# Running sums of an attention layer: carried in PSUM as float32r parts, and taken along one sequence

## The reference

```python
pos_values = x @ Wpv + bpv
pos_mem_cos = cumsum(cos(pp) * pos_values, axis=1)          # pp: phases of the position, the same for both sequences
pos_mem_sin = cumsum(sin(pp) * pos_values, axis=1)
pos_ret = (cos(pp) * pos_mem_cos + sin(pp) * pos_mem_sin) / sqrt(D)
key_ph = tanh(x @ Wk + bk) * pi
gates = sigmoid(gelu(concat([x, shift1(x)]) @ Wg1 + bg1) @ Wg2 + bg2)
kv_mem_cos = cumsum(shift1(cos(key_ph)) * (x @ Wkv + bkv) * gates, axis=1)
kv_mem_sin = cumsum(shift1(sin(key_ph)) * (x @ Wkv + bkv) * gates, axis=1)
kv_ret = (cos(key_ph) * kv_mem_cos + sin(key_ph) * kv_mem_sin) / (sqrt(max(cumsum(gates), 1)) * sqrt(D))
blended = bw[0] * pos_ret + bw[1] * kv_ret                   # bw: softmax of a small network of x
out = x + layernorm(blended) @ Wo + bo                       # x here: layernorm of the input; then
x1 = x_in + layernorm(out)                                   # ... the layer's residual
```

## Time and profile before

| | |
|---|---|
| median of 3 runs | 3562.35 us |
| the profiled execution | 3565.71 us, of which its span 3563.9 us |
| PE busy in the span | 3177.3 us (89%) |
| DVE busy | 3086.5 us (87%) |
| ACT busy | 2120.2 us (59%) |
| POOL busy | 1935.4 us (54%) |
| first phase | from 0 to about 799.5 us of the span |

### The profile page before, as it was taken

The page is one execution under the profiler, slowest core; times in us unless marked ns, Lnnn a source line. Parts: engine busy times, 40 slices in busy tenths (PEclk is TensorE's granted clock), DMA queues, the critical chain, the costliest instruction groups (busy, mean ns, idle before and its releaser), DMA issues. The chain is left out here.

```text
span 3563.9 us, 91251 instructions
## 1 busy us (share of the span) xinstructions
PE 3177.3 (89%) x31284; PEld 2733.0 (77%) x31284; DVE 3086.5 (87%) x15020; ACT 2120.2 (59%) x4411; POOL 1935.4 (54%) x1758
## 2 busy tenths in 40 slices
PE   5999999972599999999999999999999999999988
PEld 3666666642488888888888888888888888888878
DVE  5666666656999999999999999999999999999971
ACT  3444444422666666666666766666666666766662
POOL 1333333333466666556556666666556656666664
PEclk9999999986699988988888999889998888999988
DMA  2111111103333333333333333333333333333332
GB/s 64 48 54 54 54 54 54 42 30 133 141 117 117 116 105 114 122 105 105 105 105 118 125 119 119 117 108 105 124 112 105 105 105 115 124 124 117 114 117 95
DMA packets 132328, 356.85 MB, mean 100 GB/s; under 512 B 13865, under 2 KB 61609, under 8 KB 129452
## 3 DMA queue, kind: packets, MB, share of 16 engines
q1 hardware_dynamic: 131868, 351.03, 30.3%
HBM read 309.01 MB, written 25.17 MB: 94 GB/s over the span
## 5 line engine op out<-in xcount | busy, mean ns | idle before, releaser
L1209 PE MATMUL b_ps_a<-b_wup,b_hid 128*128 128x256 f32 x4096 | 955.8, 379 | 1.5 <-POOL b_hid L1023 1.5
L1198 PE MATMUL b_ps_h<-b_xT_hi,b_wd_split 128*128 128x256 f32 x4096 | 931.9, 311 | 22.7 <-ACT b_hid L1349 22.5
L1209 PEld LDWEIGHTS b_ps_a<-b_wup,b_hid 128*128 128x128 f32 x4096 | 744.3, 190 | 85.7 <-POOL b_hid L1023 1.7
L1023 POOL TENSOR_TENSOR b_hid<-b_hid,b_gates 128x512 f32<-128x512 f32 x512 | 661.9, 1295 | 197.8 <-ACT b_hid L1349 197.8
L1198 PEld LDWEIGHTS b_ps_h<-b_xT_hi,b_wd_split 128*128 128x128 f32 x4096 | 703.5, 200 | 38.3 <-issue 27.9
L1328 ACT ACTIVATE b_ohq<-b_q_no,b_minus_qid 80x128 f16<-80x128 f16 x2048 | 648.7, 391 | 1.0
L1004 POOL TENSOR_SCALAR b_rstd<-b_mv 128x2 f32<-128x2 f32 x64 | 136.4, 2131 | 860.8 <-DVE b_mv L1388 860.8
L1123 PE MATMUL b_ps_s<-b_ohr,b_ohq 80*128 80x32 f16 x16384 | 452.6, 185 | 167.1 <-issue 125.5
L1198 PE MATMUL b_ps_h<-b_xT_lo,b_wd_split 128*128 128x256 f32 x2048 | 596.9, 291 | 0.0
L1123 PEld LDWEIGHTS b_ps_s<-b_ohr,b_ohq 80*128 80x128 f16 x16384 | 443.8, 102 | 176.0 <-issue 132.3
L1349 ACT ACTIVATE b_hid<-b_ps_h 128x512 f32<-128x512 f32 x512 | 303.8, 593 | 371.5 <-PE b_ps_h L1198 371.3
(11 more groups left out here) (192 smaller groups left out, 5508.8 us busy)
## 6 DMA issues: line engine op xcount, KB each, us to landing
b_wd_split<-wd_parts SPq DMA_DIRECT2D x512, 512.0 KB, 3.8
a_keysh<-a_key SPq DMA_DIRECT2D x16, 896.0 KB, 5.4
a_x<-in_x SPq DMA_DIRECT2D x16, 512.0 KB, 4.9
x_between<-a_y SPq DMA_DIRECT2D x16, 512.0 KB, 3.2
b_x<-x_between SPq DMA_DIRECT2D x32, 256.0 KB, 2.7
wd_parts<-b_wd_split SPq DMA_DIRECT2D x16, 512.0 KB, 2.9
b_x1t<-x_between SPq DMA_DIRECT2D x32, 256.0 KB, 5.5
out<-b_y SPq DMA_DIRECT2D x32, 256.0 KB, 5.6
```

The lines of the kernel that those rows point to most:

```text
L1023: G.tensor_tensor(hid[:, p % 4, :, :], hid[:, p % 4, :, :], gates[:, 2 * p:2 * p + 2, :], ALU.mult).then_inc(mix_done, 1)
L1198: mm = T.matmul(hbank[p % 2][:, j * C:(j + 1) * C], a, c, start=i == 0, stop=i == len(parts) - 1)
L1209: mm = T.matmul(abank[:, t * D:(t + 1) * D], hid[:, p % 4, j, t * P:(t + 1) * P], wup[:, 2 * p + j, :], start=p == 0 and j == 0 and t == 0 ...
```

## The change

- The sums stay in PSUM along a sequence. For each tile `sums` adds to `cbank` first the rows that the tile before left out (`rest`, the matrix ones - tri, times that tile's terms), then its own (`upto`, a copy of tri): together these make the running sum. Both are float32r, and so are the terms, in two parts: `u_hi`, made on ACT by `high_terms` (a copy of 128x1024), and `u_lo` = u - u_hi, made on POOL by `low_terms`. That makes 8 float32r matmuls of 512 columns for a tile (4 for the first of a sequence) in place of 4 float32 ones. `keep_carry` and `carry` go; `back` now waits for `sums` itself.
- The chunks go along sequence 0 and then sequence 1. The phases are loaded, reduced and turned into sines for every chunk instead of every second one.
- The first values and terms of the next chunk, `values(n + 1, 0)` and `terms(n + 1, 0)`, stand ahead of `sums(n, 3)` and `back(n, 3)`. `norm_out` and `add_input` of chunk n - 2 stand early in the loop's turn n (they stood at the end of turn n - 1). `reduce_phases(n + 1)` stands behind `back(n, 0)`; on SP the phases of chunk n + 1 are loaded behind the load of x for chunk n + 2. Some smaller steps move too: `norm_in`, `moments_in`, the second half of `gate_values` (now `gate_shares`), `turn_blend` ahead of `key_waves` on ACT.

The diff, cut to its core (new semaphores, the changed indices of slots, and the waits that only follow from them are left out):

```diff
-        for b in range(seqs):
-            G.memset(keysh[0:1, b, 0, :, :], 0.0)
-        G.memset(zeros[:, :], 0.0)
-        G.memset(carry[:, :, :], 0.0).then_inc(constants, 1)
+        G.memset(key_end[:, :, :, :], 0.0)
+        G.memset(zeros[:, :], 0.0).then_inc(constants, 1)
...
-        j, b = divmod(n, seqs)
+        b, j = divmod(n, per_seq)
...
         def load_phases(n):
-            j = n // seqs
-            if n % seqs == 0:
-                if j:
-                    sp.wait_ge(cs_done, j)
+            j = n % per_seq
+            if n:
+                sp.wait_ge(cs_done, n)
...
             if has(n + 2):
                 if n + 2 > 0:
                     load(n + 2)
-                load_phases(n + 2)
             if has(n + 1):
+                load_phases(n + 1)
                 shift_keys(n + 1)
             if has(n - 1):
                 store(n - 1)
...
+        def low_terms(n, t):
+            g = n * TA + t
+            i = g % 2
+            pool.wait_ge(u_hi_done, g + 1)
+            G.tensor_tensor(u_lo[:, i, :], u[:, i, :], u_hi[:, i, :].bitcast(F32), ALU.subtract).then_inc(u_lo_done, 1)
...
-        for n in range(-2, chunks + 1):
+        for n in range(-2, chunks + 2):
+            if has(n):
+                low_terms(n, 1)
+            if has(n - 2):
+                add_input(n - 2)
             if has(n - 1):
                 root(1, n - 1)
             if has(n):
                 gather_terms(n, 0)
+                low_terms(n, 2)
             if has(n + 2):
                 root(0, n + 2)
             if has(n):
                 gather_terms(n, 1)
+                low_terms(n, 3)
                 gather_terms(n, 2)
+            if has(n + 1):
+                low_terms(n + 1, 0)
             if has(n - 1):
                 root(2, n - 1)
             if has(n):
                 gather_terms(n, 3)
             if has(n + 1):
                 gate_root(n + 1)
-            if has(n - 1):
-                add_input(n - 1)
...
         def sums(n, t):
-            pe.wait_ge(u_done, g + 1)
+            first = g % (per_seq * TA) == 0
+            pe.wait_ge(upto_done, 1)
             if g:
                 pe.wait_ge(prod_done, g)
-            for h in range(2):
-                mm = T.matmul(cbank[h][:, :], tri[:, :], u[:, i, h * 512:(h + 1) * 512], start=True, stop=first)
             if not first:
                 for h in range(2):
-                    mm = T.matmul(cbank[h][:, :], last_row[:, :], carry[:, b, h * 512:(h + 1) * 512], start=False, stop=True)
+                    for part in (u_hi, u_lo):
+                        mm = T.matmul(cbank[h][:, :], rest[:, :], part[:, (g - 1) % 2, h * 512:(h + 1) * 512], ...)
+                mm.then_inc(rest_pe, 1)
+            pe.wait_ge(u_lo_done, g + 1)
+            for h in range(2):
+                for part in (u_hi, u_lo):
+                    mm = T.matmul(cbank[h][:, :], upto[:, :], part[:, g % 2, h * 512:(h + 1) * 512], ...)
             mm.then_inc(sums_pe, 1)
...
     PE:   values(n, 1); turn_x(n + 1); sums(n, 0); keys(n + 1); values(n, 2); sums(n, 1); values(n, 3);
           gating(n + 1); turn_blend(n - 1); logits(n + 1); sums(n, 2); project_out(n - 1);
+          values(n + 1, 0);
           sums(n, 3); gate_sums(n + 1)
...
     ACT:  turn_x(n + 1);
-          keep_carry(n, 0); keys(n + 1); keep_carry(n, 1); gating(n + 1); key_waves(n + 1); turn_blend(n - 1);
-          gate_exp(n + 1); keep_carry(n, 2); keep_carry(n, 3); waves(n + 1)
+          high_terms(n, 1); keys(n + 1); high_terms(n, 2); gating(n + 1); turn_blend(n - 1); key_waves(n + 1);
+          high_terms(n, 3); gate_exp(n + 1); waves(n + 1); high_terms(n + 1, 0)
...
     DVE, of the changed kernel:
+          terms(n, 1); turn_x(n + 1); blend(n - 1, 3); norm_out(n - 2); gate_factors(n); blend_moments(n - 1);
+          back(n, 0); reduce_phases(n + 1); blend_norm(n - 1); terms(n, 2); moments_in(n + 2); back(n, 1);
+          blend(n, 0); terms(n, 3); norm_in(n + 2); blend(n, 1); gate_values(n + 1); back(n, 2);
+          gate_shares(n + 1); blend(n, 2); project_out(n - 1); terms(n + 1, 0); back(n, 3); gate_sums(n + 1)
```

More of the change, by code:

```diff
@@ L52, in attention_phase @@
     T, V, S, G = nc.tensor, nc.vector, nc.scalar, nc.gpsimd
-    chunks = seqs * length // CA
+    per_seq = length // CA
+    chunks = seqs * per_seq
     ident, tri, last_row, ones = (sb(f"a_{n}", [P, P]) for n in ("ident", "tri", "last_row", "ones"))
+    upto, rest = (sb(f"a_{n}", [P, P], F32R) for n in ("upto", "rest"))
     wproj = sb("a_wproj", [P, 2, KD, 3 * D], F32R)
@@ L88, in attention_phase @@
     u = sb("a_u", [P, 2, 4 * D])
-    carry = sb("a_carry", [P, seqs, 4 * D])
+    u_hi, u_lo = (sb(f"a_{n}", [P, 2, 4 * D], F32R) for n in ("u_hi", "u_lo"))
     prod = sb("a_prod", [P, 2, 2, 2, D])
@@ L138, in attention_phase @@
         sem(f"a_{n}") for n in ("w_high", "xT_hi", "x_before", "tanh", "th_abs", "key"))
[L139 to L143, removed]
+    hidden_done, exp_done, u_hi_done, lnT_done, ph_abs_done, cs_done = (
+        sem(f"a_{n}") for n in ("hidden", "exp", "u_hi", "lnT", "ph_abs", "cs"))
+    xT_pe, keys_pe, hidden_pe, logits_pe, gcum_pe, values_pe, rest_pe, sums_pe, lnT_pe, wo_pe = (
+        sem(f"a_{n}_pe") for n in ("xT", "keys", "hidden", "logits", "gcum", "values", "rest", "sums", "lnT", "wo"))
     N_WEIGHTS = 16
@@ L545, in act_program @@
             if has(n):
-                keep_carry(n, 1)
+                high_terms(n, 2)
             if has(n + 1):
                 gating(n + 1)
-                key_waves(n + 1)
             if has(n - 1):
@@ L552, in act_program @@
             if has(n + 1):
+                key_waves(n + 1)
+            if has(n):
+                high_terms(n, 3)
+            if has(n + 1):
                 gate_exp(n + 1)
-            if has(n):
-                keep_carry(n, 2)
-                keep_carry(n, 3)
             if has(n + 1):
                 waves(n + 1)
+                high_terms(n + 1, 0)
     def dve_program(dve):
+        dve.wait_ge(weights_in, 16 * N_WEIGHTS)
+        V.tensor_copy(upto[:, :], tri[:, :])
+        V.tensor_tensor(rest[:, :], ones[:, :], tri[:, :], ALU.subtract).then_inc(upto_done, 1)
         dve.wait_ge(w_high_done, 1)
@@ L745, in norm_out @@
             op.then_inc(norm_done[2], 1)
-        for n in range(-2, chunks + 1):
+        for n in range(-2, chunks + 2):
             if has(n):
-                terms(n, 0)
                 terms(n, 1)
+            if has(n + 1):
+                turn_x(n + 1)
             if has(n - 1):
                 blend(n - 1, TA - 1)
-            if has(n + 1):
-                turn_x(n + 1)
+            if has(n - 2):
+                norm_out(n - 2)
             if has(n):
@@ L760, in dve_program @@
                 back(n, 0)
-            if has(n + 2):
-                moments_in(n + 2)
-                reduce_phases(n + 2)
+            if has(n + 1):
+                reduce_phases(n + 1)
             if has(n - 1):
@@ L773, in dve_program @@
                 terms(n, 3)
+            if has(n + 2):
+                norm_in(n + 2)
+            if has(n):
                 blend(n, 1)
@@ L778, in dve_program @@
                 back(n, 2)
+            if has(n + 1):
+                gate_shares(n + 1)
+            if has(n):
                 blend(n, 2)
@@ L781, in dve_program @@
                 project_out(n - 1)
+            if has(n + 1):
+                terms(n + 1, 0)
             if has(n):
@@ L785, in dve_program @@
                 gate_sums(n + 1)
-            if has(n - 1):
-                norm_out(n - 1)
     with nc.Block() as block:
```

97 lines of the change are left out of this document (49 added, 48 removed).

## The result

The changed kernel takes 3664.96 us (median of 4 runs, 3664.28 to 3672.38) against 3561.54 us (median of 4, 3560.12 to 3564.18) for the kernel before: a ratio of 1.0294, 95% interval 1.0276 to 1.0312. It is slower by 103 us; 3653 was predicted, with 3575 to 3705 as the range. Of the four executions of the kernel with the phases loaded earlier one took 3812.38 us at a mean granted clock of 0.749; it counts in no ratio.

The account below looks back on a forecast made before the run. TensorE bounds the first phase until a chain across other engines is longer. 13 turns at 7.9 make +103, start and end -12: 3656.7 us, 3.4 less against the median, 3653; range 3575 to 3705.

Parts of the forecast that it names:

- The saving on PE: Sums on PE: four tiles save 4 x 1.7 = 6.8 us a chunk, leaving 37.3 with the hole closed.
- Steps 2 to 6: Chain from the end of high_terms(n,3) to the first Gelu of gating(n+2): 9.6, 7.2, 5.7, 6.9 and 11.4 us.
- step 1: Third gating group on PE, then third Gelu, turn_blend, key_waves and high_terms(n,3) on ACT: 9.0 us.
- The term of the clock: PE at 1.2 GHz after idling: third gating group 1.5 us longer, turn_blend held up by 0.5.
- The other signs: Turns of 50 to 55 us; DVE idle for the phases in 13; ACT awaits terms, PE the Gelu, SP add_input.
- The lock: Ports shared by DVE and POOL: 0.7 us where low_terms(n+1,1) meets norm_out; as a rival 3700 to 3725, chance 0.12.
- step 4: On POOL gate_root, low_terms(n+1,1) and add_input(n-1): 5.7 us, together 31.5.
- The rival that wanted 57 to 59 a turn: Each low_terms on POOL holds DVE's steps up to 2.35 us, PE colder: 3700 to 3725, chance 0.12.
- Start and end: First norm_in -5.9 us, first turns at PE's pace -8 and -2, open latencies at the end +4: together -12.
- The transfer isn't waited for: Phases already there for DVE when back(n+1,0) ends: 43.4 us a turn, 3523 in all, chance 0.12.
- PE stays the bound: First phase at PE's pace, 37.3 to 38.5 us a turn: 3452 in all, chance 0.05.
- step 6: On DVE reduce_phases(n+2), blend_norm, terms(n+1,2), then on ACT high_terms(n+1,2), table load and Gelu: 11.4 us.

Follow-up runs that it names:

- the last experiment: Changed kernel with terms(n,2) and phases early, low parts on DVE, and gate_factors, gate_sums, low_terms(n,0) moved on DVE: 3479.17 us, 0.9767 to the kernel before.
- the last two kernels: Changed kernel with terms(n,2) and phases early, low parts on DVE: 3516.57 us; the same with gate_factors, gate_sums, low_terms(n,0) moved on DVE: 3479.17 us.
- both cuts: Changed kernel with SP's phases load ahead of the store and ACT's gating and key_waves ahead of high_terms(n,2): 3663.66 us, 1.0282 to the kernel before.

## Why the prediction was right, point by point

- *TensorE bounds the kernel before.* Held: less PE work gave 54 us there. That "less work there pays until a chain across the other engines is longer" decided the case: that chain was only 3 us behind.
- *The saving on PE.* Held. In the warm stream the eight float32r matmuls of a tile start 0.23 us apart (404.89 to 406.52), 1.87 us with the last, against 1.92 predicted and the 3.63 of the earlier trace rows. PE's 37.3 a turn shows in the last experiment. The saving was real and lay off the path.
- *Steps 2 to 6.* All five came out within 0.2 us in the turn of the table. But the measured steps hold their handoffs (0.08 from the end of ACT's cast at 453.61 to POOL's subtraction at 453.69), for which the prediction had 1.0 more: that term wasn't needed. It made up for a step 1 that was 0.6 too short, so that 53.4 against 53.34 is in part luck. The landing is 6.0 in the median (4.7 to 6.8) against 5.9 in the earlier trace rows; the wait for it occurs in 13 turns, as counted.
- *Step 1.* The term of the clock was the weakest. PE idles 4.3 ahead of the third gating group, which then takes 2.93 in place of 1.5, and the eight transposes 1.91 in place of 1.04; so far as predicted. Not foreseen: in half of the turns `logits` also runs at 1.2 GHz (its groups of four take 0.99 in place of 0.58), `sums(n,3)` stands behind it, and `high_terms(n,3)` waits 1.75 for its `rest` half (the row at 452.57). Those turns have 12.65 against 11.0, the others 10.3 to 10.8, and the mean, 11.6, hides it.
- *PE's idle time.* 14 us a turn was predicted, most of it ahead of the third gating group. It is some 10, as PE at the lower clock is busy for some 43 and not 37.3; 3.9 of it stand ahead of that group and 4.2, more than anywhere else, ahead of `sums(n,1)`, a wait that the prediction doesn't have. So the sign "PE below 80% busy" missed narrowly: 82% from 100 to 796 us (568.95 of 696), at a clock of 0.85. The other signs came.
- *The lock.* Taken as 0.7 on the path, which came out at 0.6 (step 4). For DVE it is much more: `norm_out` takes 3.44 beside `low_terms(n,1)` (1.38 for the like step in the earlier trace rows), and the 4-column copy 2.36 beside `add_input`:

```profile
415.77 3.44 DVE L618 TENSOR_SCALAR a_y<-a_y,a_mv,a_rstd 128x256 f32<-128x256 f32 x4
416.31 2.43 POOL L253 TENSOR_TENSOR a_u_lo<-a_u,a_u_hi 128x1024 fp32r<-128x1024 f32 x1
...
419.30 2.36 POOL L263 TENSOR_TENSOR a_y<-a_y,a_x 128x1024 f32<-128x1024 f32 x1 [0.55 <-DVE a_y L618]
419.33 2.36 DVE L667 COPY a_fac<-a_z 128x4 f32<-128x4 f32 x1
```

  The copy is issued 0.03 behind the addition and ends with it; alone it takes 0.17. In sum DVE is busy for 40 a turn where its work in the kernel before is 32. The rival that wanted 57 to 59 a turn for this fell all the same: these holds end ahead of the wait for the phases, and taking the largest away changed nothing. They cost once that wait is gone: the last two kernels lie 37 us apart, though the last also moves `gate_sums` and a subtraction, so that not all of it need be the holds. The Trainium skill, "SBUF — State Buffer", "Who interferes with whom", says that whoever issues first gets the shared ports for the whole instruction; these rows agree, and so does the first pair of the earlier trace rows; its last row, POOL's scaling of 128x256, stays the exception.
- *Start and end.* This term was mis-sized: -12 predicted, some -3 measured (98.6 of span, less 13 x 7.84 = 102); it is the larger part of the 12 us by which 3653 fell short. The first `norm_in` did come 6 us earlier (first `logits` done at 53.2 against 59.0 us), but I set the next turns, at PE's new pace, against 45.5 us. The kernel before has turns of 34.4 and 43.0 there itself (58.98, 93.43, 136.44, against 53.19, 91.19, 129.75), so that they gave 1 us in place of 8 to 10. And by the first store the lead of 7 us was gone (156.35 against 156.27): `norm_out` and `add_input` of a chunk now stand in the next turn, which the term doesn't count; that this took the lead is likely, and no run shows it. It was an average taken where it didn't hold.
- *The rivals.* "The transfer isn't waited for" and "PE stays the bound" are excluded by the wait in 13 turns and by the run with half of the sums. The order of the transfers is a cause: moving that issue alone gave back 67 us. But the rival's price for an unwaited transfer, 43.4 a turn, was too low: it was 47.8, as the other steps don't fall away with it.

My expectations behind the prediction were poorer where I cut the ring in one place and didn't walk the queues again: with the Gelus moved ahead I had 3530 to 3560 for both cuts, and got 3664.

One more row on the path: the table load ahead of the Gelu starts 0.02 us behind the end of the cast and takes 1.28, and the Gelu follows at once, at 440.27:

```profile
437.92 1.04 ACT L505 CAST a_u_hi<-a_u 128x1024 fp32r<-128x1024 f32 x1 [19.05 <-DVE a_u L633]
438.98 1.28 ACT L520 ACT_TABLE_LOAD   x1
```

The Trainium skill, "ScalarE: Activation LUTs", "What ACT_TABLE_LOAD costs", gives the load about 1.28 and a drain of about 1.38 beside it. By that step 6 would be 1.4 longer; the load agrees, and the trace shows no drain here.

What stays open: which link is the last one in the kernel with the early terms and phases (45.0 a turn), and whether the two lengths of turn would become one if PE were given work in its hole; neither was tried.

## What to carry to other kernels

When work on the fullest engine is replaced by smaller pieces that pass through three others, walk the ring from one event of a turn to the same event of the next, through every in-order queue and every transfer that waits behind it; if the walk is longer than a turn, the saving is not to be had in that order. Once a ring is found, look for the cheapest link to cut, and walk it again with the cut made, for a step that is moved out of one chain usually holds another. A saving that first measures as a loss can be real: here the same cheaper sums were 2.9% slower in one order and 2.3% faster in another, with their subtractions on another engine.

## What the runs showed of the hardware that I had not expected

- Turns of one and the same program come in two lengths, as 52 at a granted clock of 0.87 and 54 to 55 at 0.81. In each of them PE has idled over 3 us ahead of its third gating group (3.39 in the shorter, 4.32 in the longer shown), and the length of that wait doesn't tell the two apart: a wait of 4.89, the longest, stands in a turn with a short step 1.
- A subtraction of 128x1024 float32 into float32r takes 2.39 us on GpSimd and 1.22 on VectorE. Four of these moved to VectorE left it less busy than before (38.9 against 40.8 us a turn). On GpSimd one such subtraction, from 409.36 to 411.75, holds a VectorE `tensor_scalar` of 4 columns from 409.49 to 411.77, 2.28 us.
- A VectorE copy of 4 columns takes 0.17 us, and 2.36 with GpSimd's addition ahead of it.
